# Flamingo layer with routed experts: new order tables, and a second bank for the experts' transposes

## The reference

```python
x = x + jnp.tanh(g_xattn[0]) * _L0_xattn_ref(_layernorm(x, axis=-1), ctx_1024, ctx_1024, Wq, bq, Wk, bk, Wv, bv, Wo, bo)
x = x + jnp.tanh(g_ffn[0]) * _L0_ffn_ref(_layernorm(x, axis=-1), router_w, router_b, expert_w, expert_b)
# attention: softmax(Q K^T / sqrt(32)) V per head, then @ Wo.T + bo
# ffn: p = softmax(xt @ router_w + router_b); e = argmax(p)
#      y = max(p) * (xt @ expert_w[e] + expert_b[e])
```

## Time and profile before

| | us |
|---|---|
| median of 3 runs | 1155.17 |
| lowest, highest | 1147.08, 1158.91 |
| the profiled execution, as timed | 1151.26 |
| its span, first to last instruction | 1149.5 |

### The profile page before, as it was taken

One profiled execution on the slowest core, in us unless ns is written; L12 is line 12 of the kernel. 1 busy time (PEld: TensorE's weight loads), 2 busy tenths in 40 slices (PEclk: granted clock), 3 DMA queues, 4 the chain that ended last, 5 costly groups with the idle time before them and its releaser, 6 DMA issues. The chain is left out here.

```text
span 1149.5 us, 19046 instructions
## 1 busy us (share of the span) xinstructions
PE 1021.9 (89%) x5464; PEld 650.7 (57%) x5464; DVE 804.2 (70%) x1748; ACT 513.6 (45%) x920; POOL 671.0 (58%) x446
## 2 busy tenths in 40 slices
PE   3788899989998999899999999999899765889985
PEld 2554566546754674476457655755565323666764
DVE  5655756877696669767975896688667758687554
ACT  4244643563456345534544454445443425333431
POOL 3046655774487448745873686557545646555553
PEclk9898999999999999999999999999999967899998
DMA  7324232523252334333423442243223722444431
GB/s 233 76 75 119 69 80 70 141 77 98 66 140 78 89 84 129 75 84 85 138 66 84 108 124 79 72 119 102 77 64 88 234 102 83 156 130 147 137 123 54
DMA packets 70884, 119.39 MB, mean 104 GB/s; under 512 B 17854, under 2 KB 18878, under 8 KB 70656
## 3 DMA queue, kind: packets, MB, share of 16 engines
q1 hardware_dynamic: 62496, 98.96, 31.4%
q0 software_dynamic: 6240, 18.68, 5.3%
q10 hardware_dynamic: 2048, 0.53, 0.2%
HBM read 50.42 MB, written 18.66 MB: 60 GB/s over the span
## 5 line engine op out<-in xcount | busy, mean ns | idle before, releaser
L691 ACT ACTIVATE probs<-sc 128x512 f32<-128x512 f32 x512 | 279.3, 598 | 205.2 <-PE sc L499 163.1
L1101 POOL TENSOR_TENSOR psum_keys<-psum_keys,probs 128x1024 f32<-128x1024 f32 x128 | 303.8, 2387 | 109.8 <-ACT probs L691 109.6
L826 DVE TENSOR_REDUCE maxima<-jb 128x1 f32<-128x512 f32 x512 | 322.5, 680 | 61.2 <-PE jb L519 60.4
L1101 POOL TENSOR_TENSOR psum_keys<-probs 128x1024 f32<-128x1024 f32 x64 | 153.5, 2413 | 231.2 <-ACT probs L691 231.2
L519 PE MATMUL jb<-k_stack,q_stack 96*128 96x512 f32 x512 | 192.9, 430 | 25.1 <-issue 9.1
L499 PE MATMUL sc<-q_stack,k_stack 98*128 98x512 f32 x512 | 193.1, 427 | 10.1 <-DMA q_stack<-max_rows 8.3
L509 PE MATMUL hb<-probs,values 128*32 128x512 f32 x1024 | 140.4, 626 | 16.4 <-DVE heads_raw L845 7.9
L519 PEld LDWEIGHTS jb<-k_stack,q_stack 96*128 96x128 f32 x512 | 95.5, 193 | 101.2 <-issue 40.3
L499 PEld LDWEIGHTS sc<-q_stack,k_stack 98*128 98x128 f32 x512 | 95.1, 193 | 83.5 <-ACT probs L691 29.9
L861 DVE SCALAR_TENSOR_TENSOR k_lo<-jb,bias,k_hi 128x512 fp32r<-128x512 f32 x32 | 23.9, 747 | 64.0 <-ACT k_hi L710 64.0
L667 PE MATMUL sc<-e_hi,heads_hi 128*128 x156 | 67.4, 432 | 1.0 <-issue 0.5
(11 more groups left out here) (230 smaller groups left out, 1883.0 us busy)
## 6 DMA issues: line engine op xcount, KB each, us to landing
k_stack<-k_hi SPq DMA_DIRECT2D x256, 64.0 KB, 2.0
q_stack<-q_hi SPq DMA_DIRECT2D x256, 64.0 KB, 2.0
stage<-in_x SPq DMA_DIRECT2D x63, 256.0 KB, 3.0
stage<-in_ctx_t SPq DMA_DIRECT2D x32, 256.0 KB, 3.0
k_stack<-k_lo SPq DMA_DIRECT2D x128, 64.0 KB, 2.0
q_stack<-q_lo SPq DMA_DIRECT2D x128, 64.0 KB, 2.0
e_lo<-in_ew SPq DMA_DIRECT2D x8, 1024.0 KB, 12.3
rows<-row SPq DMA_DIRECT2D x30, 257.5 KB
```

Source lines behind the costliest of these rows:

```text
L691: nc.scalar.activation(probs[:, kt % 2, h, :], scs[(16 * g + n) % NSC][:], ACT.Exp, scale=SCALE)\
L826: nc.vector.tensor_reduce(maxima[g % 2][:, n:n + 1], jbs[j][:], AX.X, ALU.max).then_inc(s["mx_done"], 1)
L1101: nc.gpsimd.tensor_tensor(psum_keys[:, two, :], in0, probs[:, kt % 2, two, :], ALU.add)\
```

## The change

All tables of orders are new, on all engines. Beside that, `TO` alternates between two banks, `hb` and `jb3`, and waits for `LO n-2` where it waited for `LO n-1`; in `CLOSING` the other steps turn through three `jb` banks. No operation is added or left out. Of the tables the diff below keeps those parts that the prediction speaks of.

```diff
 ORDER = {
     "PE": [
...
-        "1P3 1SUM 2S0 2S1 3M0 2S2 3M1 2S3 3M2 2S4 2S5 2S6 3M3 2S7 3M4 3M5 3M6 2S8 ^T4 2S9 2P0 2S10 3M7 3M8 2P1 ^T5 3M9",
-        "2S11 2S12 3M10 3M11 2P2 2S13 3M12 ^T6 ^T7 3M13 3M14 2S14 3M15 ^0Q ^0Qb ^0Qc ^0Qd 3MT ~RT3 ^0K 2S15 ^0Kb ^0Kc 3S0",
-        "^0Kd 3S1 3S2 3S3 2SUM 2P3 3S4 3S5 3S6 ~RL1 3S7 3P0 3S8 3S9 ^0M0 ^0M1 ^0M2 3S10 ^0M3 3P1 ^0M4 ^0M5 ^0M6 3S11 ^0M7",
...
+        "2MT ~RT2 1P2 1P3 2S0 2S1 1SUM 2S2 2S3 3M0 2S4 3M1 3M2 3M3 2S5 2S6 2S7 3M4 3M5 2S8 ^T4 2P0 2S9 3M6 2S10 2S11 3M7",
+        "3M8 3M9 ^T5 2S12 3M10 3M11 2P1 2P2 ^T6 3M12 ^T7 2S13 2S14 3M13 3M14 3M15 ^0Q ^0Qb ^0Qc ^0Qd 3MT ~RT3 ^0K 2S15",
+        "^0Kb ^0Kc 3S0 ^0Kd 3S1 ~RL1 2P3 3S2 3S3 2SUM 3S4 3S5 3S6 3S7 3S8 3P0 ^0M0 ^0M1 ^0M2 ^0M3 3S9 3P1 ^0M4 3S10 ^0M5",
     ],
...
     "DVE": [
...
-        "2M15 ~OP2 2MT ~LR2 ~OP3 ~LR3 ^LX0 ^LX1 0NL 1SC 3M0 3M1 3M2 3M3 1NM 3M4 3M5 3M6 ^LX2 ^T4 3M7 3M8 ^LX3 3M9 W6 ^T5",
-        "3M10 3M11 3M12 ^T6 ^T7 3M13 3M14 3M15 W2 ^0Q 3MT ^0K 1NL 2SC 2NM ~RS1 ^0M0 ^0M1 PC ^0M2 ^0M3 ^0M4 ^0M5 ^0M6 ^0M7",
...
+        "2M10 2M11 2M12 2M13 2M14 ~OP2 ~LR2 2M15 ~OP3 2MT ~LR3 ^LX0 0NL ^LX1 1SC 3M0 3M1 3M2 1NM 3M3 ^LX2 3M4 3M5 3M6 ^T4",
+        "3M7 3M8 ^LX3 3M9 3M10 ^T5 3M11 3M12 ^T6 ^T7 3M13 3M14 3M15 ^0Q 3MT 1NL ^0K ~RS1 2SC 2NM ^0M0 ^0M1 ^0M2 PA ^0M3",
     ],
...
 LAST = {
     "PE": [
...
-        "3M0 ~OP3 ~OPb3 ^T4 3M1 ~OPc3 ~RT2 ^T5 ^0Qb 2S2 ~OPd3 3M2 ^T6 ^0Qc 2S3 1SUM ^0K 2S4 2S5 2S6 2S7 ^0Kb 3M3 2S8 3M4",
-        "2S9 ^Vc0 3M5 2S10 ^0Qd 3M6 ^Vd0 2P0 3M7 3M8 2S11 2S12 3M9 2P1 2S13 3M10 3M11 2S14 2S15 3M12 3M13 2P2 3M14 ~RT3",
...
+        "~OPb3 2S0 2S1 1SUM ~OPc3 ~OPd3 2S2 ~RT2 ^0Qb 3M0 2S3 2S4 2S5 3M1 2S6 2S7 ^V0 ^0Qc 3M2 ^0K ^Vb0 2S8 3M3 2P0 3M4",
+        "3M5 3M6 2S9 ^0Qd 2P1 3M7 ^Vc0 ^T5 ^Vd0 2S10 2S11 3M8 3M9 2S12 3M10 ^0Kb 3M11 ^0Kc 3M12 2S13 3M13 2S14 3M14 3M15",
+        "2S15 3MT 2P2 ~RT3 ^0M0 ^0M1 2P3 3S0 3S1 3S2 ^0Kd 3S3 3S4 ^1Q ^V1 3S5 3S6 ^1Qb ^0M2 2SUM 3S7 ^0M3 3S8 ~RL1 3P0",
     ],
     "ACT": [
-        "^T4 ^V1 2MT 2MD ~RT2 2E0 ^T5 ^NX0 ^0Q 0NM 2E1 ^C0 2E2 ^V2 2E3 2E4 ^C1 2E5 2E6 2E7 ^1Q 2E8 2E9 1NM 2E10 2E11 2E12",
-        "W0 2E13 3MT 2E14 3MD 2E15 ~RT3 ^0MT 3E0 3E1 3E2 3E3 3E4 ^2Q 3E5 ^C2 3E6 3E7 3E8 3E9 3E10 3E11 ^0K 3E12 3E13 2NM",
-        "^NX1 3E14 3E15 ^T6 ~RS1 ^0E0 ^0E1 ^0E2 ^3Q W1 ^0E3 ^0E4 ^0E5 ^0E6 ^0E7 ^1K ^0E8 ^1MT ^0E9 ^NX2 W6 ^0E10 ^0E11",
-        "^0E12 ^0E13 3NM ^0E14 W2 ^0E15 ^1E0 W3 W4 ^T7 NE0 W5 ^1E1 ^1E2 W7 ^0MD ^NX3 RT0 ^1MD ^V3 ^1E3 ^1E4 ^2K ^1E5 RT1",
+        "1E14 ^C1 1E15 2MT 2MD 2E0 ^V1 2E1 0NM 2E2 ^0K 2E3 2E4 2E5 ~RT2 2E6 2E7 ^V2 2E8 2E9 ^1Q 2E10 1NM 2E11 2E12 2E13",
+        "2E14 2E15 W0 ^NX0 3MT 3MD ^2Q 3E0 ^0MD 3E1 3E2 ^T4 3E3 ~RT3 3E4 ^T5 3E5 ^T6 3E6 3E7 ^C2 W1 3E8 ^1MD ~RS1 ^T7 3E9",
+        "2NM 3E10 3E11 3E12 3E13 3E14 3E15 W6 ^0E0 ^0E1 ^0E2 ^0E3 ^0E4 ^0E5 3NM ^1K ^NX1 ^0E6 ^0E7 ^0E8 ^0E9 ^0E10 W2",
+        "^0E11 ^NX2 ^0E12 ^0MT ^0E13 ^0E14 ^0E15 ^C3 ^1E0 W3 W4 ^1E1 ^1E2 ^NX3 W5 W7 NE0 ^1E3 RT0 RT1 ^2K ^3Q ^1E4 ^1E5",
     ],
     "DVE": [
-        "2M12 2M13 2M14 2M15 ~LI0 2MT 3M0 ~OP2 ^0K 3M1 ^LX3 ~OP3 3M2 0NL 1SC 1NM 3M3 3M4 3M5 ~LR2 3M6 3M7 1NL 3M8 3M9",
-        "3M10 3M11 3M12 3M13 3M14 3M15 ^T6 ^0M0 3MT ^0M1 ^0M2 ^0M3 ^0M4 ^0M5 ^1Q ^0M6 ^0M7 ~LR3 ^0M8 2SC ^0M9 ^0M10 W0",
-        "^0M11 2NM ~RS1 ~RC1 ^0M12 ^0M13 ~LI1 ^0M14 ~RG1 ^0M15 ^1M0 ^1M1 2NL ^1M2 ^1M3 ^1M4 ^1M5 W1 PA 3SC 3NM ^1M6 W6",
-        "^1M7 PC ^1M8 ^0MT ^1M9 ^1M10 ^2Q 3NL ^1M11 ^1M12 W2 ^1K OP0 LR0 OP1 LR1 ^1M13 ^T7 ^1M14 ^1M15 ^2K",
+        "~LR0 ~OP1 ^T4 1M14 ~LR1 1M15 1MT 2M0 2M1 2M2 ~RS0 0SC ~RC0 0NM 2M3 3Q 2M4 ~RG0 2M5 2M6 3K 2M7 2M8 2M9 2M10 ^0Q",
+        "2M11 2M12 2M13 2M14 2M15 2MT ~LI0 ~OP2 1SC ~OP3 0NL 3M0 3M1 1NM 3M2 3M3 ~LR2 3M4 3M5 3M6 3M7 ^T5 3M8 3M9 3M10",
+        "3M11 3M12 ^LX0 ^0K 3M13 3M14 3M15 ^0M0 ^0M1 ^T6 ^0M2 3MT 1NL ~LR3 2SC ^0M3 ^0M4 ^T7 ^0M5 ^0M6 ^0M7 ^0M8 2NM ^LX1",
+        "^0M9 ^0M10 ^0M11 ^0M12 ^0M13 ^LX2 ^0MT ~RS1 ^0M14 ~RC1 ^0M15 ^1M0 ^1M1 ^1M2 W0 ^1M3 ~RG1 ~LI1 ^1M4 2NL ^1M5 ^1M6",
+        "^1M7 ^1M8 PA ^1Q 3SC ^1M9 3NM ^1M10 ^1M11 ^1M12 ^2Q W1 W6 3NL PC ^1K ^1M13 ^1M14 W2 OP0 ^1M15 OP1 LR0 ^2K LR1",
     ],
...
 CLOSING = {
     "PE": [
-        "~OP0 ~OPb0 ~OPc0 ~OPd0 ~OP1 ~RT0 ~OPb1 ~OPc1 ~OPd1 ~OP2 ~OPb2 ~OPc2 ~OPd2 TO0 ~RT1 ~OP3 ~RT2 ~OPb3 ~OPc3 ~OPd3",
-        "~RL0 TO1 Y0 TO2 ~RC0 Y1 TO3 ~RT3 Y2 TO4 Y3 TO5 ~RL1 TO6 Y4 TO7 Y5 TO8 Y6 ~LI0 TO9 Y7 ~RC1 TO10 Y8 TO11 Y9 ~LI1",
-        "TO12 Y10 TO13 Y11 TO14 Y12 Y13 SB TO15 Y14 TO16 Y15 TO17 Y16 TO18 Y17 TO19 Y18 TO20 Y19 TO21 Y20 TO22 Y21 TO23",
+        "~OP0 ~OPb0 ~OPc0 ~OPd0 ~OP1 ~RT0 ~OPb1 ~OPc1 ~OPd1 ~RT1 ~OP2 ~OPb2 TO0 ~OPc2 ~OPd2 TO1 ~OP3 ~OPb3 TO2 ~OPc3",
+        "~OPd3 ~RL0 ~RT2 Y0 Y1 ~RT3 ~RC0 TO3 Y2 TO4 TO5 Y3 Y4 TO6 ~RL1 Y5 TO7 Y6 TO8 Y7 TO9 ~RC1 ~LI0 Y8 TO10 Y9 ~LI1",
+        "TO11 Y10 TO12 TO13 Y11 TO14 Y12 SB Y13 TO15 TO16 Y14 Y15 TO17 Y16 TO18 Y17 TO19 Y18 TO20 Y19 TO21 Y20 TO22 Y21",
     ],
     "ACT": [
-        "NE1 HI0 HI1 NE2 NE3 HI2 ~RS0 ~RT2 HI3 NE4 ~RT3 HI4 NE5 NE6 HI5 HI6 NE7 NE8 HI7 HI8 NE9 HI9 NE10 HI10 NE11 HI11",
+        "HI0 NE1 HI1 NE2 ~RS0 HI2 NE3 HI3 NE4 ~RT2 NE5 HI4 HI5 ~RT3 NE6 NE7 HI6 NE8 HI7 HI8 NE9 HI9 NE10 HI10 NE11 NE12",
     ],
     "DVE": [
-        "W3 ~OP2 W7 ~RS0 LO0 ~OP3 ~LR2 LO1 LO2 FI0 FI1 ~RG0 LO3 LO4 ~LR3 FI2 LO5 FI3 LO6 ~RC0 LO7 FI4 FI5 LO8 ~RS1 FI6",
+        "W3 W7 LO0 ~OP2 ~LR2 LO1 ~RS0 ~RG0 ~OP3 LO2 ~LR3 FI0 LO3 FI1 LO4 FI2 LO5 ~RC0 FI3 LO6 ~RS1 FI4 LO7 FI5 LO8 FI6",
     ],
...
@@ -203,10 +203,10 @@
 
     found = {}
     for b, table in bodies():
-        turn = 0
+        turn, turns = 0, NJB - 1 if b == B else NJB
         for (_, _, kind, _), item in zip(tokens_of(table, "PE"), items_of(table, "PE", b)):
             if kind in THROUGH_JB:
-                found[item] = turn % NJB
+                found[item] = turn % turns
                 turn += 1
     return found
 
@@ -380,6 +380,7 @@
         scs = [ps(f"sc{i}", [P, S]) for i in range(NSC)]
         hb = ps("hb", [P, S])
         jbs = [ps(f"jb{i}", [P, S]) for i in range(NJB)]
+        turned = hb, jbs[NJB - 1]
 
         s = {n: sem(n) for n in (
             "w_in0", "w_in1", "w_in2", "w_in3", "c_in0", "c_in1", "rb_in", "bo_in", "w_hi_done",
@@ -647,10 +648,12 @@
                 elif kind == "TO":
                     if n == 0:
                         wait(pe, s["nm_chain"], NG * B)
+                    elif n == 1:
+                        jb_free(NJB - 1)
                     pe.wait_ge(s["xe"], n + 1)
-                    wait(pe, s["lo"], n)
+                    wait(pe, s["lo"], n - 1)
                     for k in range(NF):
-                        last = nc.tensor.transpose(hb[:, k * P:(k + 1) * P], xe[n % 2][:, k * P:(k + 1) * P], ident[:])
+                        last = nc.tensor.transpose(turned[n % 2][:, k * P:(k + 1) * P], xe[n % 2][:, k * P:(k + 1) * P], ident[:])
                     last.then_inc(s["tp"], 1)
                 elif kind == "Y":
                     if n == 0:
@@ -786,7 +789,7 @@
                     act.wait_ge(s["tp"], n + 1)
                     wait(act, s["op_mm"], NT * (B - 1) + min(n + 1, NT))
                     wait(act, s["y"], n + 1 - WORK)
-                    nc.scalar.activation(xt_hi[n % WORK], hb[:, :].rearrange("p (k q) -> p k q", q=P), ACT.Copy)\
+                    nc.scalar.activation(xt_hi[n % WORK], turned[n % 2][:, :].rearrange("p (k q) -> p k q", q=P), ACT.Copy)\
                         .then_inc(s["hi"], 1)
 
             for b, table in bodies():
@@ -1054,7 +1057,7 @@
                     nc.vector.tensor_tensor(dst_b, jbs[j][:, 0:LATE], bad, ALU.add).then_inc(s["plan_ready"], 1)
                 elif kind == "LO":
                     dve.wait_ge(s["hi"], n + 1)
-                    nc.vector.tensor_tensor(xt_lo[n % WORK], hb[:, :].rearrange("p (k q) -> p k q", q=P),
+                    nc.vector.tensor_tensor(xt_lo[n % WORK], turned[n % 2][:, :].rearrange("p (k q) -> p k q", q=P),
                                             xt_hi[n % WORK].bitcast(F32), ALU.subtract).then_inc(s["lo"], 1)
                 elif kind == "FI":
                     dve.wait_ge(s["eb_in"], 16)
```

More of the change, by code:

```diff
@@ L34 @@
     "SP": [
-        "~~RW2 ~~RW3 1SQ ^DC0 1SK 2SQ 2SK ^DC1 ~RW0 ^DC2 ^DC3 ~RW1 ~DR2 ~DR3 3SQ ^DX0 ^DX1 ^DX2 3SK ^DX3 DR0 DR1 ^0SQ",
-        "^0SK",
+        "^DC0 ^DC1 ^DC2 ^DC3 ~RW0 ~DR2 ~RW1 ~DR3 3SQ ^DX0 ^DX1 ^DX2 3SK ^DX3 DR0 ^0SQ ^0SK DR1 ^1SQ ^1SK ~RW2 ~RW3 ^2SQ",
+        "^2SK",
     ],
     "PE": [
[10 rows of a table removed]
[10 rows of a table added]
     ],
     "ACT": [
[5 rows of a table removed]
[5 rows of a table added]
     ],
     "DVE": [
[5 rows of a table removed]
[5 rows of a table added]
     ],
     "POOL": [
-        "C3 ~1A3 ~~OP2 ~~OP3 ~1A4 ~1A5 LX0 ~2A0 LX1 ~2A1 LX2 LX3 ~2A2 ~OP0 ~2A3 ~2A4 ~2A5 ~~LR1 ~3A0 ~3A1 ~3A2 ~3A3 ~3A4",
-        "~3A5 ~OP1 0A0 0A1 0A2 0A3 0A4 0A5 ~LR0 1A0 1A1 ^C0 ^C1 ^C2 1A2",
+        "~~3A4 ~~3A5 ~0A0 ~0A1 ~0A2 ~0A3 ~~OP0 ~~OP1 ~0A4 ~0A5 ~~LR0 ~1A0 ~1A1 C0 C1 C2 ~1A2 ~1A3 ~~OP2 C3 ~~OP3 ~1A4",
```

(15 more changed lines are left out.)

2 lines of the change are left out of this document (1 added, 1 removed), and 92 rows, old and new, of tables (CLOSING, LAST, OPENING, ORDER).

## The result

The changed kernel takes 1183.2 us in the median of four runs, beside 1155.5 us for the kernel before: ratio 1.025, with an interval of 1.019 to 1.031. A later set of runs, on another occasion and with both kernels side by side again, gave 1.015 (1.012 to 1.018). I had forecast 1126 us, a gain of 29; it lost 28.

The account below looks back on a forecast made before the run. PE's list was taken as the bound wherever it isn't made to wait. Last stage 14, experts 9, sequences 0 to 6 6 and opening 0 sum to 29 us: 1155.2 - 29 = 1126 us, range 1110 to 1145.

Parts of the forecast that it names:

- Sequences 0 to 6: Middle sequences: fewer changes of kind and fewer SUM waits, less a longer P3.0 wait, 0.9 us each: 6 us gained.
- `SUM`'s waits: PE in each middle sequence: 1.2 us of waiting for POOL goes, since S or P is placed ahead of SUM1 and SUM2.
- The change of kinds: PE's list of one sequence: neighbouring matmuls of unlike kind fall from 47 to 42, 0.5 us gained a sequence.
- Last stage: Finishing the last sequence and preparing the experts, up to Y0: 14 us gained, by NL1 and its train (10) and W0 (3.9).
- The first part: Last stage up to MT3: NL1 behind M3 and MT3 on DVE, MT3 counted at 916 instead of 926 us.
- the second part: Last stage up to NM2: W0 moves behind RC1 on DVE, 3.9 us less; NM2 at 927.4 instead of 941.33.
- The third part: Last stage from NM2 to Y0: OP0 keeps its distance and POOL's list from PC to Y0 holds the same work; no gain.
- Experts: Experts' stage: all 6.9 us of TO's waits for LO go and 2 us of a late HI: 9 us gained.
- Opening: Start of the kernel: the first matmul comes some us later, but Q's wait for T7 ends sooner; 0 net.
- The rival of the slower middle sequences: NM2 comes 5 us later in every sequence, P3.0 waits and the clock may drop: 1167 us; chance 0.07.
- The rival of the collisions that only move: Last stage: DVE operations again held through several POOL additions, with half of the experts' gain: 1141 us; chance 0.17.

Follow-up runs that it names:

- e15: Kernel before with MT2 behind OPd3 on PE, MT2 behind LR2, M2.15 and OP3 on DVE, and SUM1 behind S2.1: 1163.3 us, ratio 1.014.
- e5: Changed kernel with NL3 moved in DVE's middle table from behind M1.7 to ahead of Q2: 1161.2 us, ratio 1.012 to the kernel before.
- e7: Changed kernel with both NL3 moved ahead of Q2 and group 2's MT put back on PE and DVE: 1148.6 us, ratio 1.000 to the kernel before.
- e16: e14 with SUM1 behind S2.0 and SUM2 behind P2.3 in the middle table: 1146.7 us, ratio 0.999 to the kernel before.
- e6: Changed kernel with group 2's MT put back where it had been on PE and DVE: 1157.8 us, ratio 1.007 to the kernel before.
- e8: e7 with, on ACT, K1 ahead of MD0 as before: 1144.8 us, ratio 0.996 to the kernel before.
- e12: Kernel before's OPENING and ORDER, changed LAST, CLOSING and two banks, with W0, LI1, PA, PC, NL3 and TO2 moved: 1137.4 us, ratio 0.988 to the kernel before.
- e14: e12 with RG1 behind RS1, OP0 and OP1 behind one W each, and W1, NL2, SC3, NM3 ahead of PA on DVE: 1137.9 us, ratio 0.991.
- e1: Kernel before with all its tables and only the second bank for TO: 1157.3 us, ratio 0.999 to the kernel before.
- e4: Kernel before's OPENING and ORDER with the changed LAST, CLOSING and two banks: 1155.2 us, ratio 0.997 to the kernel before.
- e2: Kernel before's OPENING, ORDER and LAST with the changed CLOSING and two banks: 1159.1 us, ratio 1.002 to the kernel before.
- e10: The kernel of e2 run again on another chip: 1142.4 us, ratio 0.992 to the kernel before.
- e3: Kernel before with the changed LAST, keeping its OPENING, ORDER, CLOSING and one bank: 1155.8 us, ratio 0.997 to the kernel before.

## Why the prediction was wrong, point by point

**Sequences 0 to 6: the step that failed.** I forecast 6 us gained and measured 32.5 and 34.5 lost; my lower bound was a loss of 14. Three things were wrong in it. First, I looked for new waits only behind `RS1`, that is at `P3.0`. This wait did grow, from 0.3 to 0.6 us, where I had put 1.1. But I didn't compare, for each DMA and each handed-over bank, how many microseconds of PE's work stand between its producer and its consumer in the two lists. For `MT2` to `S2.0` they fell from 5.2 us to 2.6, against a path of 4.1. The diff shows it, and e15, which takes that stretch alone into the kernel before, loses 16 us; moving `MT2` back gains 12.6 us from e5 to e7. Second, the 1.2 us of `SUM`'s waits were entered as a gain, as if PE then had less to wait for. e16 shows them as the cheaper of two waits: removed, they cost 9 us. Third, "so this costs next to nothing in sequences 0 to 6" read the median of `NL` as a promise for the new order too; `NL3` now collided in six of the seven sequences, since a table that is used again and again repeats its collision. It costs PE 1.02 us of waiting in each of the six; e7 gains 9 us on e6 (4 to 11) by moving it. With `K1`, the moves bring the end of sequence 6 back by 16 to 23 of the 32.5 to 34.5 us; the rest stays open.

The size was wrong also because I priced waits at their own length. In some of the sequences the clock fell to 0.50 behind PE's pauses, and 17.9 us more of waiting came with 14.7 us more of busy time, 32.6 in all.

**The change of kinds.** 0.5 us a sequence for 42 instead of 47 neighbours of unlike kind was not tested by itself, and the traces don't settle it. In sequences of e8 with a clock of 1.00 PE is busy for 106.6 us; the kernel before has 106.9 to 107.3 in the later set, but 106.6 and 106.8 in two sequences of the first.

**Last stage.** Forecast 14 us, measured 5.9 and 7.2. The first part was right: `MT3` came 9.2 us sooner behind the end of sequence 6 (10 forecast), as `NL1`'s train of maxima is gone. Of the second part nearly nothing came: `NM2` is 10.2 us sooner, not 13.9, since `W0`'s 3.9 us were taken up by `S3.0`, which waits 2.83 us for its maxima. ACT's `W0` stands ahead of its half of `MT3`. I had seen this hole, put it at 2 us and set it against the 2.40 that goes; but then it sits on the path on which I counted `W0`'s gain. The third part was called neutral and lost some 4: `NM2` to `PC` took 29.5 us where it took 27.2 (and `NM2` to `OP0` 31.8 for 30.1), with `PA` at 8.29 us beside POOL's additions where it had 6.18, and `PC` to `Y0` 22.2 where it took 20.3 (20.5 for 20.3 in the later pair). That `W1`, `W6` and `NL3` stand between `NM3` and `PC`, and that POOL's whole list waits for `PC`, was in the lists; I wrote "it comes in DVE's list just before `W2` and `OP0` as it did".

**Experts.** Forecast 9 us. With the signals in time, 4.9 in the traces and 10 (6 to 14) in the timed runs, for the bank and the new `CLOSING` together: the waits for `LO` went as forecast, and the size fits in the timed runs and is half in the traces. In the pair of traces that the forecast started from, 5.4 us were lost. The 3.9 us that I called a late `HI` and counted as half recoverable, with its like, was one of the late signals (the kernel before has two in its first trace), and these grew.

**Opening.** Right, and for the reason given: the first matmul came 4.5 us later (15.9 us) and the end of the list at 80.4 instead of 79.8.

**Rivals and chances.** The rival of the slower middle sequences had the right place and, for the later set, nearly the right time (1167; 1183 and 1169 measured), by a mechanism, `P3.0` behind `RS1`, that played no part. It got 0.07 since I took the rest of the new middle table as equal. The rival of the collisions that only move is right in what it says (`NL3`, `PA`, `NL1` all met additions), but the collisions alone make a small part of the loss. The sentences on what would show me wrong named the waits of `P3.0` and of `TO`; they left out `S2.0`, whose DMA was in no step.

The Trainium skill (SBUF — State Buffer, Who interferes with whom) has the blocked instruction wait for the one that holds the port. The changed kernel's rows agree with that better than the earlier trace rows do: `NL3` takes 2.67 us, from 538.80 to 0.56 us behind the end of one addition. Why `NL1` waited through three in the kernel before stays open; it did so in all six traces with the old `LAST` (7.24 or 7.25 us). Nothing in the sums above rests on it.

## What to carry to other kernels

When the order of a pipelined list changes, go through each pair of a producer and a consumer that has a latency of its own (a DMA, a bank, a split on two engines) and add up the work that stands between them, before and after: a pair that loses cover is a new wait, however many old ones the change removes. In a list that is repeated, multiply by the repetitions, and look whether the clock falls behind the pauses: here it nearly doubled the loss (17.9 us of waiting, 32.6 in all). A visible short wait is not a gain yet; ask what stands next behind it.

## What the runs showed of the hardware that I had not expected

Even the smallest operation can be held: in e12, 8 values a partition took 2.32 us beside an addition of POOL (951.06 to 953.59). The same operation takes 0.16 us in e14, where POOL does nothing beside it, and a neighbour of the same size in e12 0.17.

```profile
951.30 2.32 DVE L993 SCALAR_TENSOR_TENSOR early_room<-numbers,counts 128x8 f32<-128x8 f32 x1
...
956.19 0.17 DVE L997 TENSOR_TENSOR_SCAN early_room<-ones,early_room 128x8 f32<-128x8 f32 x1
```

PE's semaphore events in the experts' stage came up to 8 us late (8.2 in e1), several at once, while its matmuls went on. It happened in all six traces of the first pair and of e1 to e4, and only during or just behind rows of gathers and scatters that POOL issued back to back (eight in a row around the wait at 1116.0). In the other groups, on two other chips, rows of 14 passed with no such wait, so the row of transfers alone is not the cause. What differs between the groups, the chip or something else, could not be settled. The stage was longer with it by 14.1 us in the changed kernel, by 13.3 in that of e2 and e10, and by 3.8 in the kernel before; e3, which has one bank, took 156.0 us, so two banks aren't needed for it. A comparison of two kernels that depends on it (ratio 1.002 in one group and 0.992 in another for the same kernel) needs more than one chip.
